# In the last cross attention, the reciprocal of the softmax sums writes 256 values on VectorE in place of 16, the copy that spread them on GpSimd goes, and on ScalarE the exponential is put ahead of a tile copy

## The reference

```python
x = x + jnp.tanh(g_xattn[i]) * attention_i(_layernorm(x), ctx_1024, ...)
x = x + jnp.tanh(g_ffn[i]) * feed_forward_i(_layernorm(x), ...)
```

```python
Q = (Q_decoder @ Wq + bq).reshape(b, sd, NUM_HEADS, D_K).transpose(0, 2, 1, 3)
K = (K_encoder @ Wk + bk).reshape(b, se, NUM_HEADS, D_K).transpose(0, 2, 1, 3)
V = (V_encoder @ Wv + bv).reshape(b, se, NUM_HEADS, D_K).transpose(0, 2, 1, 3)
scores = jnp.einsum('bhqd,bhkd->bhqk', Q, K) / math.sqrt(D_K)
attn = jax.nn.softmax(scores, axis=-1)
out = jnp.einsum('bhqk,bhkd->bhqd', attn, V)
out = out.transpose(0, 2, 1, 3).reshape(b, sd, d)
return out @ Wo + bo
```

## Time and profile before

| | |
|---|---|
| median of 3 runs | 3300.7 us (3300.07 to 3302.83) |
| the profiled execution | 3300.07 us, its span 3298.8 us |
| granted TensorE clock, mean | 0.975 |
| busy, share of the span | PE 94%, DVE 56%, ACT 36%, POOL 19% |
| chain that ended last | PE 81%, DVE 8%, ACT 5%, POOL 2%, DMA 2%, issue 3% |

### The profile page before, as it was taken

How to read it: one execution, slowest core, us unless ns; L and a number is a source line. 1 busy time by engine, 2 the same in 40 slices (tenths; PEclk the granted TensorE clock), 3 DMA queues, 4 the chain that set the end, 5 groups by cost and what they waited for, 6 DMA issues and landing times.

```text
span 3298.8 us, 40142 instructions
## 1 busy us (share of the span) xinstructions
PE 3100.2 (94%) x15356; PEld 2157.3 (65%) x15356; DVE 1856.9 (56%) x3029; ACT 1183.8 (36%) x2206; POOL 620.0 (19%) x998
## 2 busy tenths in 40 slices
PE   7999999999999999999999999879998889996996
PEld 5667867677767776776666666556666655555664
DVE  5996778558756875685311101693317757764113
ACT  4443323552254235422221222241224436662331
POOL 1306400100100010001100000250343222111554
PEclk8999999999999999999999999998999989997998
DMA  5200000010002000200100000002461011112633
GB/s 134 66 1 1 29 26 1 13 47 20 1 13 67 1 1 14 65 1 1 38 13 13 26 0 0 20 1 102 145 209 46 4 46 50 34 41 96 214 123 107
DMA packets 85395, 151.03 MB, mean 46 GB/s; under 512 B 26357, under 2 KB 62743, under 8 KB 80471
## 3 DMA queue, kind: packets, MB, share of 16 engines
q1 hardware_dynamic: 70327, 77.15, 7.6%
q0 software_dynamic: 14880, 71.33, 6.2%
HBM read 173.14 MB, written 17.56 MB: 58 GB/s over the span
## 4 chain that ended last, share of the span: by engine, by line
PE 81%; DVE 8%; ACT 5%; issue 3%; POOL 2%; DMA 2%; SPq 0%; ACTq 0%; DVEq 0%; POOLq 0%
PE psum L408 10%; PE psum L431 9%; PE psum L1748 7%; PE psum L1736 7%; PE psum L1410 7%; PE psum L1422 6%; PE psum L2237 6%; PE psum L2258 3%; PE psum L444 2%; PE psum L1105 2%; PE psum L2412 2%; PE psum L2841 2%; PE psum L396 2%; PE psum L716 2%; PE psum L2862 1%
## 5 line engine op out<-in xcount | busy, mean ns | idle before, releaser
L408 PE MATMUL psum<-Vt,shared 128*128 128x256 f32 (+1 forms) x1600 | 366.3, 384 | 13.2 <-ACT shared L571 12.0
L431 PE MATMUL psum<-Kt,xnTt 128*128 128x512 f32 (+1 forms) x960 | 343.9, 508 | 0.5 <-ACT xnTt L516 0.5
L408 PEld LDWEIGHTS psum<-Vt,shared 128*128 128x128 f32 (+1 forms) x1600 | 298.8, 191 | 69.4 <-issue 31.6
L431 PEld LDWEIGHTS psum<-Kt,xnTt 128*128 128x128 f32 x960 | 179.4, 189 | 158.6 <-issue 153.4
L1422 PEld LDWEIGHTS psum<-expert_w,prep 128*128 128x128 f32 x1024 | 194.6, 190 | 78.1 <-issue 57.9
L1422 PE MATMUL psum<-expert_w,prep 128*128 128x256 f32 x1024 | 240.8, 379 | 0.0
L1410 PE MATMUL psum<-weights,expert_w 128*128 128x512 f32 x512 | 240.3, 593 | 0.0
L3097 DVE TENSOR_REDUCE row<-psum 128x1 f32<-128x128 f32 (+7 forms) x256 | 186.7, 755 | 92.3 <-PE psum L2843 91.8
L1310 DVE SCALAR_TENSOR_TENSOR bias<-Kt,small,bias 128x1232 f32<-128x1232 f32 x96 | 149.2, 1554 | 129.7 <-ACT Kt L1294 128.4
L1768 ACT ACTIVATE prep<-psum,fside 128x512 f32<-128x512 f32 x128 | 88.0, 687 | 345.0 <-PE psum L1736 344.9
L1796 DVE TENSOR_TENSOR inner<-psum,inner 128x512 f32<-128x512 f32 x56 | 36.1, 686 | 308.2 <-PE psum L1748 308.2
(11 more groups left out here) (418 smaller groups left out, 6192.6 us busy)
## 6 DMA issues: line engine op xcount, KB each, us to landing
expert_w<-in_L_xattn_Wf SPq DMA_DIRECT2D x16, 512.0 KB, 5.5
weights<-q_parts SPq DMA_DIRECT2D x32, 144.0 KB
weights<-k_parts SPq DMA_DIRECT2D x96, 48.0 KB
weights<-in_L_xattn_Wk SPq DMA_DIRECT2D x4, 1024.0 KB, 4.9
weights<-in_L_xattn_Wv SPq DMA_DIRECT2D x4, 1024.0 KB, 7.0
weights<-in_L_xattn_Wq SPq DMA_DIRECT2D x4, 1024.0 KB, 5.4
weights<-in_L_xattn_Wo SPq DMA_DIRECT2D x4, 1024.0 KB, 5.4
weights<-in_L_ffn_w SPq DMA_DIRECT2D x8, 512.0 KB, 4.5
```

What stands on the lines that cost most here:

```text
L408: ins = pe.matmul(o_bank(t), probT[0:rows, t % 2, c, :], Vt[0:rows, t // TB, c, :], start=(c == 0), stop=(c == CH - 1))
L431: ins = pe.matmul(flat[:, par * 3 * BANK + at:par * 3 * BANK + at + cols], xnTt[:, par, k, :], Kt[:, t // TB, k, src:src + cols], start=(k ...
```

## The change

The DVE reciprocal of this stage reads the 16 sums of a row broadcast to 256 and writes `wide_shares` itself. It signals `shares_made`, and PE's transposes wait for that. The copy on POOL and its waits are gone; in their place DVE waits, from tile 2 on, for PE's transposes of tile t-1 (`p_turned`), which are the last to read the half of `wide_shares` that is written again. DVE's wait for POOL before the sum is gone as well. In ACT's queue `power(t + 1)` now stands ahead of `keep_tile(t + 3)`, as it does already in the stage with `feed`.

```diff
     def pe_turn_shares(pe, t):
-        pe.wait_ge(weights_made, 6 * NT + t + 1)
+        pe.wait_ge(shares_made, NT + t + 1)
...
         dve.wait_ge(powered, g + 1)
-        if n == 6 and t >= 2:
-            dve.wait_ge(weights_made, g - 1)
         dve.tensor_reduce(total, Pb, AX.X, ALU.add).then_inc(dve_step, 1)
         dve.wait_ge(dve_step, vs())
+        if n == 6:
+            if t >= 2:
+                dve.wait_ge(p_turned, 3 * g)
+            dve.reciprocal(wide_shares[:, par, :, :], total.unsqueeze(2).to_broadcast([P, H, HD])).then_inc(shares_made, 1)
+            return
         if not divide:
             dve.reciprocal(total, total).then_inc(shares_made, 1)
             return
...
         for t in range(NT):
             keep_probabilities(t)
-            if not feed and t + 3 < NT:
-                keep_tile(t + 3)
             if t + 1 < NT:
                 power(t + 1)
-            if feed and t + 3 < NT:
+            if t + 3 < NT:
                 keep_tile(t + 3)
...
             par = t % 2
             Pb = prob[:, par, :].rearrange("p (h c) -> p h c", h=H)
-            shares = row[:, par, H:2 * H].unsqueeze(2)
             if n == 5:
                 pool.wait_ge(shares_made, NT * (n - 5) + t + 1)
-                pool.tensor_tensor(Pb, Pb, shares.to_broadcast([P, H, S2]), ALU.mult).then_inc(weights_made, 1)
+                pool.tensor_tensor(Pb, Pb, row[:, par, H:2 * H].unsqueeze(2).to_broadcast([P, H, S2]), ALU.mult).then_inc(weights_made, 1)
             pool.wait_ge(normed, NT * n + t + 1)
             pool.tensor_tensor(x[:, t, :], x[:, t, :], gated_bo, ALU.add).then_inc(bo_added, 1)
-            if n == 6:
-                pool.wait_ge(shares_made, NT * (n - 5) + t + 1)
-                if t >= 2:
-                    pool.wait_ge(p_turned, 3 * (NT * n + t))
-                pool.tensor_copy(wide_shares[:, par, :, :], shares.to_broadcast([P, H, HD])).then_inc(weights_made, 1)
```

## The result

| | before | after |
|---|---|---|
| median of 5 runs | 3300.07 us (3297.66 to 3302.83) | 3318.21 us (3314.62 to 3321.79) |
| profiled execution, its span | 3300.07, 3298.8 us | 3321.63, 3320.4 us |
| first sum of the stage to the start of the next stage | 119.29 us | 138.80 us |

The ratio is 1.0055, with a 95% interval from 1.0041 to 1.0070: the changed kernel is slower, by 18 us. The forecast was 3320, range 3311 to 3327.

The account below looks back on a forecast made before the run. The prediction took PE as the bound of the last attention stage, with DVE close behind. 24.0 us of reciprocals - 10.1 of old waits + 5.6 of remaining waits = 19.5 us, giving 3320 us, range 3311 to 3327.

Parts of the forecast that it names:

- The reciprocal, 1.75 us: On DVE, the reciprocal grows from 16 to 256 results: 1753 ns each, 24.0 us more over 16 tiles.
- d: Growth of one DVE reciprocal per tile, taken as 1.50 us.
- The waits that hide: DVE's five waits for PE before the residual at even tiles 6 to 14: 10.1 us before, 5.6 us after.
- S: The start of DVE's sum in a tile, from which the prediction counts its times.
- Part 2: POOL's 16 copies of 0.40 us go, off the path: gain 0; DVE's changed waits also 0.
- Part 3: On ACT the exponential precedes the turned tile's copy, delaying PE's projection and the residual; alone, 3.0 us.
- S4 to S5: The step from the start of tile 4's sum on DVE to that of tile 5's.
- Sum, 19.5 us: Whole stage: 24.0 for the reciprocals, less 10.1 of old waits, plus 5.6 of remaining waits.
- Rival 3: PE's clock falls as PE idles more: once, about +3.5 us, 3323, chance 0.12; in every pair, 3337, chance 0.04.
- Rivals 1, 2 and 4: Reciprocal cheap, 3305, chance 0.09; moved copy costs nothing, 3315, chance 0.13; reciprocal a third dearer per element, 3325, chance 0.04.
- rival 2: ACT's moved copy costs nothing as PE has slack: 24.0 - 10.1 + 1 = 14.9 us, 3315; chance 0.13.

Follow-up runs that it names:

- the lengths experiment: The kernel before with eight additional DVE instructions ahead of the stage, reciprocals of 32 to 256 elements and one copy of 256; 3304.47 us in one run.
- the runs where no residual waits: The changed kernel with ACT's order as before, 3312.2 us; and the changed kernel with PE's output product of odd tiles ahead of the scores, 3312.34 us.
- the fillers: The changed kernel with multiplications without use on PE, 15 ahead of tile 15's transposes and 8 between these and the output product; drain 13.51 us.
- the one with the move alone: The kernel before with only ACT's order changed, the exponential ahead of the copy of the turned tile; 3302.13 us, ratio 1.0007.
- the 0.27%: The kernel before with PE's output product of odd tiles put ahead of the scores; 3289.88 us, ratio 0.9973.
- the run with the short reciprocal: The changed kernel, but DVE inverts the 16 sums in place and a DVE copy spreads them to 256; 3305.93 us, ratio 1.0026.
- the run with 15 fillers: The changed kernel with 15 multiplications without use on PE ahead of the transposes of tile 15; 3316.12 us, ratio 1.0052.

## Why the prediction was right, point by point

- *The reciprocal, 1.75 us, d = 1.50.* 1753 ns, all 16; the lengths experiment shows the line up to there. Neither figure taken from the Trainium skill (VectorE: DVE Perf Modes) holds for it: 8 cycles an element, which is the prediction's estimate from the repeat count (Walkthrough, the fixed hardware budget), would be 8.33 ns, the formula (N + 151)/0.96 (TRN2 errata section), which the page gives for the float32 addition of two tensors, 1.04 ns; the rows show 6.25, and they decide. The formula's fixed part is 151 cycles, 157 ns, near the 153 of the rows and not equal to it, as the prediction has it. 15 of them lie between the first and the last sum, 22.5 us, the sixteenth in the drain.
- *The waits that hide.* Forecast 10.1 falling to 5.6, measured 4.45. At tiles 8, 10 and 14 they are 1.00, 1.00 and 1.32 us (forecast 1.05, 1.05 and 1.38): the moved copy starts 0.1 us before the exponential ends, so the queries start at S + 1.47 and not S + 1.6 (2562.86 - 2561.39), and DVE is ready 0.08 us earlier too. At tiles 6 and 12 they are 0.37 and 0.76, because there the sum before (tiles 5 and 11) came 0.65 and 0.28 us late while the copy on ACT did not: the wait covers DVE's delay. Each of the five pairs from tile 4 to 14 took 15.98 or 15.99 us whatever happened on DVE, so with the moved copy the way over ACT and PE sets the pair. 22.5 - 10.1 + 4.45 = 16.8 is the measured 16.80, but that it closes to the hundredth is luck: 0.8 us that stopped or held DVE (at tiles 3 and 5, below) are not in it, and are made up by rows of before that were longer than after, the normalisations at tiles 6 and 8 (0.50 and 0.71 us for 0.41) and six divided outputs (0.69 for 0.63).
- *Part 2 at nothing.* The new wait for PE never stopped DVE. But POOL, no longer held by the sums, ran ahead, and its 3.51 us clear fell on the normalisation of tile 5, which took 1.45 us. The step from S4 to S5 took 7.93 us where 5.78 + 1.50 = 7.28 was due, so +0.65, and the wait before the next residual was 0.37 and not 1.00: the pair is 15.99 us like the others. So the forecast's zero holds in the sum, by a wait that happened to stand behind; without it, as in the runs where no residual waits, the pair was 15.79 or 15.78 us for 15.17. Before, the same clear fell on the normalisation of tile 8.
- *Part 3, 3.0 us alone.* 2.98 up to the last sum, of which 1.7 are in the waits that it was worked out from and 1.1 in a wait at tile 4 that it had at nothing. In the changed kernel 3.35 us up to the last sum are its.
- *Sum, 19.5 us.* The stage grew by 19.51. The agreement is better than the terms deserve, and in part luck: the waits were forecast 1.1 us too long, and the drain grew by 2.7 and not 1.5. The 2.7 contain the lower clock under the output product; at the full clock the drain is 12.01 us with a short reciprocal and, with the fillers, 13.51 with the long one, which is 1.50.
- *Rival 3.* By the prediction's own sign, a granted clock under 0.9 between 2510 and 2600, it happened, beside the forecast and not in place of it, and it was small. The granted clock was 0.66 in 2520 to 2525 us, behind 4.14 us without work before the projection of tile 4. It cost 0.17 us in this profile, since DVE was the bound there, and 0.2 to 1.2 in three others of the same code; the forecast had 3.5. It happened again in the drain, where it costs up to 1.9. (The 1.1 us that the prediction gives for ten transposes at the full clock is their share of the chain; in the timeline, from which the 2.09 is, they take 1.25 to 1.31.) The clock did not fall in the pairs, as the windows show, first of the idle time at tile 1, then of the middle:

```profile
2515.00:2520.00 5.00, 0.86 (x7) 0.54 (x6) 3.99 (x5) 1.49 (x2) 2.87 (x9) 1.00 0.00 0
2520.00:2525.00 5.00, 5.00 (x35) 4.83 (x37) 4.93 (x4) 1.75 (x5) 0.00 (x0) 0.66 0.00 0
```

```profile
2560.00:2600.00 40.00, 35.11 (x245) 25.48 (x244) 36.99 (x47) 18.30 (x45) 6.74 (x14) 1.00 0.00 1
```

PE was busy for 17.6 of 20 us there (17.1 forecast), DVE for 18.5.
- *Rivals 1, 2 and 4.* The reciprocal was neither cheap nor steeper, and the move was not free: 135.18 us without it, 138.80 with it. What rival 2 gave for the case without it, +14.9, was +15.9: 13.45 up to the last sum, where 13.4 was due, and 2.44 in the drain, where the product took 3.65 us.

Open is what decides the clock in the drain. Behind the same 3.05 us of idling the transposes of tile 15 and the product behind them took 2.09 and 2.69 us in the kernel before, 1.31 and 1.99 in the one with the move alone, and 2.39 and 3.56 in the lengths experiment, whose stage is the same code as before:

```profile
2609.38 2.39 PE L396 MATMUL psum<-ident,shared 128*128 128x128 f32 x10 [3.05 <-ACT shared L847]
...
2611.99 3.56 PE L740 MATMUL psum<-Vt,prep 128*128 128x256 f32 x8
```

So it differs between executions of one code, and the edits are not needed to explain it.

## What to carry to other kernels

Take a reciprocal on the smallest shape and spread its result with a copy: the work saved on a free engine is paid for by the busy one, here at 6.25 ns for each element against 0.29 us for an undisturbed copy of all 256 (0.35 in the mean). Before an instruction is moved in an idle engine's queue, look at who is queued behind its result: here the copy was early for free, and late it held PE's projection and all that PE had behind it. Where the bounding engine waits for a copy of its own last result, put independent work of its own ahead of the dependent one; that gave the 0.27% that neither kernel had.

## What the runs showed of the hardware that I had not expected

- A DVE normalisation (one float32 input and output in SBUF) did not proceed while POOL cleared a buffer. It started at 2544.02 us, POOL's clear ended at 2545.33, and it ended at 2545.47, 1.45 us for 0.41. The same clear did it in the kernel before (the normalisation from 2553.89 to 2554.60, the clear up to 2554.45) and with the short reciprocal (up to 2538.17 and 2538.03): each time the normalisation ended 0.14 or 0.15 us behind the clear. The timelines of DVE and POOL after:

```profile
2544.02 1.45 DVE L267 TENSOR_SCALAR xn<-x,meanvar,rstd 128x256 f32<-128x256 f32 x1
```

```profile
2541.82 3.51 POOL L3233 MEMSET weights<- 128x4096 bf16 x1
```

DVE's maximum (from PSUM) and shift ran through the same clear with 1.38 and 1.44 us. In the run with the short reciprocal the spreading copy took 1.17 us once while POOL worked, for 0.29.
- Behind 2.27 us in which PE idled, the product took 3.67 us for 1.99, although the transposes before the idle time had run at the full clock (the run with 15 fillers, one profile). Behind 0.49 to 0.79 us it took 1.99 or 2.00 in every profile shown here.
